# GpSimd's scatter of expert results: add to the zeroed rows in memory instead of overwriting them

## What is computed

```python
xbuf = jnp.zeros((E, C, D), dtype=x.dtype).at[e_sorted, pos].set(x[tok_sorted], mode='drop')
g = jnp.einsum('ecd,efd->ecf', xbuf, w_gate)
u = jnp.einsum('ecd,efd->ecf', xbuf, w_up)
y = jnp.einsum('ecf,edf->ecd', jax.nn.silu(g) * u, w_down)
y_pair = y[e_sorted, safe_pos] * (s_sorted * valid)[:, None]
out = jnp.zeros((N, D), dtype=x.dtype).at[tok_sorted].add(y_pair)
...
x = _layernorm(x + _L1_ffn_ref(...), axis=-1)
```

## Time and profile before

| what | us |
|---|---|
| median of three runs | 3461.25 (3458.54 to 3462.05) |
| the profiled execution | 3459.88 |
| its span in the trace | 3458.1 |
| outside the span | 1.8 |
| rows of the first turn in place, TensorE starts on them | 3051.5 |
| first send of GpSimd starts | 3066.7 |
| last send of GpSimd starts | 3415.9 |
| TensorE busy in the whole span | 3237.2 (94%) |
| GpSimd busy in the whole span | 2055.3 (59%) |

### The profile page before, as it was taken

One profiled execution on the slowest core, in us unless ns is written; L12 is line 12 of the kernel. 1 busy time (PEld: TensorE's weight loads), 2 busy tenths in 40 slices (PEclk: granted clock), 3 DMA queues, 4 the chain that ended last, 5 costly groups with the idle time before them and its releaser, 6 DMA issues. The chain is left out here.

```text
span 3458.1 us, 96150 instructions
## 1 busy us (share of the span) xinstructions
PE 3237.2 (94%) x37252; PEld 2262.0 (65%) x37252; DVE 2374.0 (69%) x4718; ACT 1947.5 (56%) x5215; POOL 2055.3 (59%) x3021
## 2 busy tenths in 40 slices
PE   9999899887899999999999999999999799879997
PEld 6777566465577777777777777777776455546665
DVE  5555477444687878787878787787778578635435
ACT  1111366422577677767776777667776377635553
POOL 3333477642566666666666666666666557657775
PEclk9999899997999999999999999999999799989999
DMA  2000554100211112111111111111110356356667
GB/s 86 17 10 13 134 132 118 34 1 17 62 54 53 43 48 58 55 46 50 52 52 43 53 49 53 44 52 49 53 43 31 88 145 177 121 201 207 213 209 258
DMA packets 229115, 278.88 MB, mean 81 GB/s; under 512 B 58420, under 2 KB 187000, under 8 KB 224024
## 3 DMA queue, kind: packets, MB, share of 16 engines
q1 hardware_dynamic: 207356, 236.71, 24.4%
q0 software_dynamic: 18432, 34.96, 2.9%
q10 hardware_dynamic: 2876, 1.06, 0.1%
HBM read 162.39 MB, written 125.83 MB: 83 GB/s over the span
## 5 line engine op out<-in xcount | busy, mean ns | idle before, releaser
L2366 PE MATMUL head_ring<-gd_xT,head_w 128*128 128x512 f32 x1024 | 508.1, 619 | 8.4 <-DMA head_w<-gd_w 5.4
L1693 POOL DMA_INDIRECT ytok<-exp_arena,exp_cur x256 | 251.2, 981 | 117.3 <-issue 73.7
L2694 DVE TENSOR_TENSOR head_Xs<-head_bx,head_join 128x512 bf16<-128x512 f32 x320 | 219.8, 687 | 81.0 <-PE head_bx L2408 81.0
L2366 PEld LDWEIGHTS head_ring<-gd_xT,head_w 128*128 128x128 f32 x1024 | 175.3, 191 | 147.4 <-issue 135.0
L2659 DVE SCALAR_TENSOR_TENSOR head_cb_V<-head_ring,head_taps,head_cb_V 128x504 f32<-128x504 f32 (+2 forms) x384 | 263.0, 726 | 2.8 <-ACT head_cb_V L2521 2.8
L2491 PE MATMUL head_by<-head_wo,head_ogT 128*128 128x256 f32 x1016 | 254.0, 393 | 6.9 <-issue 0.3
L2375 PE MATMUL head_ring<-head_w,gd_xT 128*128 128x256 f32 x1024 | 257.9, 395 | 0.0
L2491 PEld LDWEIGHTS head_by<-head_wo,head_ogT 128*128 128x128 f32 x1016 | 183.2, 190 | 37.3 <-DVE rows_xc L2727 13.7
L2375 PEld LDWEIGHTS head_ring<-head_w,gd_xT 128*128 128x128 f32 x1024 | 185.7, 191 | 32.4 <-issue 0.5
L2566 ACT CAST head_Tt<-head_btt 128x512 bf16<-128x512 f32 x320 | 194.3, 607 | 17.7 <-PE head_btt L2416 15.9
L2586 ACT COPY head_U<-head_bu 128x512 f32<-128x512 f32 x256 | 137.4, 589 | 109.8 <-PE head_bu L2454 109.8
(11 more groups left out here) (404 smaller groups left out, 9313.9 us busy)
## 6 DMA issues: line engine op xcount, KB each, us to landing
xbuf<-head_blank SPq DMA_DIRECT2D x64, 552.0 KB
exp_arena<-xbuf SPq DMA_DIRECT2D x64, 552.0 KB, 5.2
hold_place<-scan SPq DMA_DIRECT2D x64, 256.0 KB
ytok<-head_blank SPq DMA_DIRECT2D x64, 256.0 KB
moe_w<-moe_w SPq DMA_DIRECT2D x32, 384.0 KB, 3.3
hold_place<-qd SPq DMA_DIRECT2D x48, 192.0 KB
hold_place<-kd SPq DMA_DIRECT2D x48, 192.0 KB
head_w<-gd_w SPq DMA_DIRECT2D x64, 128.0 KB, 3.0
```

What stands on the lines that cost most here:

```text
L1693: pool.indirect_dma_start(ytok, bass.IndirectOffsetOnAxis(ap=cur[i % AHEAD][s][:, b:b + 1], axis=0), y[i % RESULTS][s][:, b, :], None, bou ...
L2366: last = pe.matmul(b[:, :], w[:, c, FEAT[what]], xT[:, c, n % UNITS * N:n % UNITS * N + N], start=c == 0, stop=c == DC - 1)
L2694: dve.tensor_tensor((Ti if a == 0 else Xs)[:, :, :], bx[:, :].rearrange("p (q i) -> p q i", i=SEQ), join[:, a, :].unsqueeze(1).broadcast_t ...
```

## The change

The indirect DMA of L1693 gets `compute_op=ALU.add`: each of its rows is added to the row of `ytok` that it is addressed to, instead of overwriting it. These rows hold zeros at that time, and each live row has an address of its own, so the values in `ytok` are the same afterwards. Shapes, indices, bounds check, semaphores, buffers and the order of all instructions stay as they are. The scatter to `xbuf` (L1354) stays a plain one.

```diff
@@ -1691,7 +1691,7 @@
                             pool.wait_ge(cur_ready[s], i + 1)
                             for b in range(QB):
                                 pool.indirect_dma_start(ytok, bass.IndirectOffsetOnAxis(ap=cur[i % AHEAD][s][:, b:b + 1], axis=0), y[i % RESULTS][s][:, b, :], None,
-                                                        bounds_check=ROWS * K - 1, oob_is_err=False).then_inc(sent[i % RESULTS][s], 16)
+                                                        bounds_check=ROWS * K - 1, oob_is_err=False, compute_op=ALU.add).then_inc(sent[i % RESULTS][s], 16)
                             back = 2 * i + s - 3
```

## The result

| | before | after |
|---|---|---|
| median of the runs, us | 3461.28 (3458.54 to 3462.05) | 3583.9 (3581.34 to 3589.18) |
| ratio after / before | | 1.0356 (95% interval 1.0343 to 1.037) |
| the profiled execution, us | 3459.88 | 3589.18 |
| its span, us | 3458.1 | 3587.4 |
| from first to last start of a send, us | 349.2 | 472.3 |

The change makes the kernel slower by 122.6 us, 3.6%. The profiled execution of after is the slowest of its four, 5.3 us over the median. It is 8 us behind before its experts begin, in stages that did not change: TensorE starts on the first rows at 3059.53 instead of 3051.50.

A forecast was written before the change was run, and what follows sets the result against it. Expert turns were taken as bound by TensorE (11.00 us a turn), GpSimd close behind at 10.22. GpSimd's longer sends +77.7, DMA engines nothing, closing stretch -4: +74 on 3459.88, plus 1.4 to the median, 3535 us; range 3459 to 3700.

The forecast's parts named there:

- the 0.78: Expert turns: GpSimd's slack in us a turn, TensorE's 11.00 less 10.22 for eight sends.
- Term (1): GpSimd's own work for a send at L1693: grows by 0.39 us, bounds 0 and 0.97; +77.7 us in all.
- d: Growth of GpSimd's time for one send, in us: taken as 0.39; the forecast case spans 0.13 to 0.7, chance 0.45.
- rival A: Expert turns: growth per send under 0.097 us stays hidden under TensorE's turn; 3461 to 3464 us, chance 0.25.
- What d costs: Expert turns: hidden up to 0.097 us a send; beyond, GpSimd is the bound, 426.9 us first to last start against 349.2.
- GpSimd is fed: Expert turns: GpSimd's sends run without gaps; neither landings nor ScalarE's copies are late; landing may triple first.
- TensorE's clock at nothing: Expert turns: TensorE busy 82%, and GpSimd's pace leaves 2.3 us a turn for a lower clock; cost nothing.
- Term (2): DMA engines: 0.18 us per engine and send grows to at most 0.36, no bound; cost in the turns nothing.
- Term (3): Closing stretch: read-back group 3 no longer queues behind group 2; -4 us, bounds 0 and -7.
- B: GpSimd's sends: each costs twice or more, growth 0.8 to 1.1 us; 3640 to 3683 us; with beyond, chance 0.20.
- C: Expert turns: DMA engines become the bound, adding rows at six times today's cost; 3563 us, chance 0.08.
- D: Whole kernel faster, only through the closing stretch's -4 us with growth per send under 0.1 us; chance 0.02.

The follow-up runs named there:

- n32: Kernel before with one send in eight adding (32 of 256), the rest plain: 3461.2 us, ratio 1.0004.
- lightplain_b: Kernel before with half of the down matmuls (L1542) left out, all sends plain: 3440.3 us against 3459.7, ratio 0.9950.
- rows kernel: Sends only 64 rows (blocks 0, 1) or 32 (blocks 2, 3), adding for a turn's first expert, plain for the second: 3568.3 us against the kernel before's 3625.0.
- lightadd: Changed kernel with half of the down matmuls (L1542) left out: 3663.6 us, on a chip where the kernel before took 3625.
- oob: Changed kernel with bounds check 0, so nearly every row is out of bounds and not sent: 3655.8 us against the kernel before's 3625.0, ratio 1.0073.
- fill: Kernel before, no send adding, with a small GpSimd sum on a scratch tile behind each send: 3506.6 us, ratio 1.0129.
- again: The changed kernel, unchanged, run once more: 3581.6 us, ratio 1.0354 to the kernel before.
- width: Sends 512 bytes of each row to a separate tensor, adding for a turn's first expert, plain for the second: 3510.5 us against the kernel before's 3459.7.
- n64: Kernel before with two sends in eight adding (64 in all), the rest plain: 3482.8 us, ratio 1.0060.
- n128: Kernel before with four sends in eight adding (128 in all), the rest plain: 3516.7 us, ratio 1.0158.

## Why the prediction was right, and where its size was off

Sign, mechanism and place were those of the forecast; the time lay inside the range, at +122.6 instead of +74 us.

- **What bounds the kernel.** Right: TensorE's 11.00 us a turn with GpSimd at 10.22 behind it. n32 (+0.5 us for 32 adds) and lightplain_b (-19.4 us where TensorE alone had some 33 to give) show both sides of the 0.78.
- **Term (1), the size of d: mis-sized, and the step to it failed.** It took 0.19 us as the fixed part of a send and split the other 0.78 evenly over two accesses, so that a third came to 0.39. The rows kernel shows a send of 32 rows at 0.871: nearly all of it is fixed, so there was no price for an access to be read from 0.78. The adding kind has a larger fixed part, by about 0.45, and somewhat more for each row. d is 0.568. The error in the sum is 255 x (0.568 - 0.39) = 45.4 us. That d came out well over the 0.13 at which the forecast begins was not derived: the 0.39 lay between two ends, 0 and 0.97, that were far apart, and by the little that rows cost it would have been near nothing. So the sign rests partly on luck, as the 0.45 given to the forecast and the 0.25 given to rival A say themselves.
- **What d costs: right.** 255 x (1.278 + 0.568) + 1.6 = 472.3, and the trace has 472.3.
- **GpSimd is fed: right.** Idle time is 0.30 ahead of every send; landing is 4.5 in the median and 7.8 at most, far from the 15 us it may take.
- **TensorE's clock at nothing: right in effect.** It was busy for about 39 of 50 us at 0.93 to 1.00, and lightadd at 0.84 took the same 472.4.
- **Term (2), the DMA engines: mis-sized, without effect.** 0.54 us per engine and send lies over the upper bound of 0.36 that one more pass was to cost. All engines together are busy 68%, near the 65% forecast, since the longer turn spread the rest, and a landing is no later in the median (4.5 us). The rule of the Trainium skill (Collectives: The Full Stack, "The bandwidth ceiling: the fold count and why AG ≠ RS ≠ AR"), half the rate for the second source read, falls short here: the page after has three times as many packets for these sends (144 instead of 48), and their time is 3.0 times. The number of packets alone does not make it, for oob has 144 too at 0.075 us a send.
- **Term (3), the closing stretch: -4 expected, -2.3 measured.** Last start to the issue of group 3 grew from 5.6 to 6.9 us (+1.3). From there to the first norm 15.8 became 12.5 (-3.2), since group 2 had been issued 14.7 us earlier instead of 9.6. The rest is -0.4.
- **The sum again:** 77.7 - 4 + 45.4 + 1.7 = 120.8 us, which is the 123.1 from first to last send less 2.3. The two profiled spans differ by 129.3; the other 8.5 had passed by the first send. The medians differ by 122.6.
- **The rivals.** A fell with d; the rule of the Trainium skill named there, that descriptor generation is small and that many can be emitted before the extra cost shows (DMA: Bandwidth & Descriptors, "Anatomy of one DMA — SWDGE (gpsimd) path"), agrees with the little that rows cost (0.871 to 0.973 from 32 to 128), but it says nothing of the 0.45 that the adding kind costs at any count. B needed 0.8 or more. C, the DMA engines as the bound, is excluded by fill, where no send adds and the time follows GpSimd's spacing all the same, and by oob, where no rows are moved and GpSimd still needs 476.1 us. D, faster, needed d under 0.1.

## What to carry to other kernels

An engine that is off the chain of waits may be the next bound by a hair: set its start-to-start distance times its count against the turn, not its busy share (59% on the page, 93% in the turn). Where a change makes each of many instructions longer, its cost is zero up to that slack, and what goes beyond it is paid once for each of them. When the price of a new kind of instruction is not in the trace, don't spread the old one's time over its rows, for most of an indirect DMA's time on GpSimd was the same for 32 rows as for 128; keep the doubled instruction as the bound.

## What the runs showed of the hardware

An indirect DMA of 128 rows that adds takes GpSimd 1.54 us, one that overwrites 0.97; with 32 rows 1.32 and 0.87. Rows out of bounds save neither GpSimd's time (1.542 in oob) nor packets (144 a send in oob and in after), and the DMA engines' time for an adding send of 1 KB rows, half of them live, is 0.54 us per engine against 0.18. A plain send right behind an adding one takes 1.02 us, and by the third it is 0.97 again (n32); an adding one behind plain ones takes 1.56 to 1.57. Some adding sends take 2.0 us instead of 1.54: two in after and in again, one in lightadd and in width, none in n32, n64 and n128 (at most 1.77), and in oob eleven between 3201 and 3361, the last nine a turn (15.2 us) apart; the cause was not looked for.
